# A graph network's last stage on one Trainium2 core: counts gathered one tile further ahead, and tile 0's mean and rows and the last mean transposed by TensorE

## The reference

```python
gates = softmax(x @ gate_W + gate_b)
top_v, top_i = top_k(gates, 2)
def sage_conv(h, W_l, b_l, W_r):
    aggr = segment_sum(h[src], dst) * inv_deg
    return aggr @ W_l + b_l + h @ W_r
for e in range(4):
    h = x
    for l in range(2):
        h = relu(sage_conv(h, Wl[e, l], bl[e, l], Wr[e, l]))
    expert_outs.append(h)
out = sum of the two chosen experts' h, each times its gate
```

## Time and profile before

| | |
|---|---|
| median of three runs | 757.63 us |
| lowest and highest | 754.64, 758.64 us |
| the profiled execution's own time | 759.32 us |
| its span in the trace | 757.6 us (757.57) |
| TensorE matmul busy | 722.2 us, 95% |
| VectorE busy | 434.0 us, 57% |
| ScalarE busy | 408.7 us, 54% |
| GpSimd busy | 183.4 us, 24% |
| last stage | from 482.8 us to the end |

### The profile page before, as it was taken

The page is one execution under the profiler, slowest core; times in us unless marked ns, Lnnn a source line. Parts: engine busy times, 40 slices in busy tenths (PEclk is TensorE's granted clock), DMA queues, the critical chain, the costliest instruction groups (busy, mean ns, idle before and its releaser), DMA issues.

```text
span 757.6 us, 12027 instructions
## 1 busy us (share of the span) xinstructions
PE 722.2 (95%) x3562; PEld 583.4 (77%) x3562; DVE 434.0 (57%) x1073; ACT 408.7 (54%) x927; POOL 183.4 (24%) x204
## 2 busy tenths in 40 slices
PE   5899999999999999999999999978999999999994
PEld 3589977888888887777777777756888788887783
DVE  8899889998842548522624424386444444453431
ACT  6956678776642523312413313357677767776771
POOL 4000000000000102831100100226555555655511
PEclk9999999999999999999999999999999999999997
DMA  9000001111501447799698692499434994439940
GB/s 214 27 3 3 4 3 32 37 34 46 158 2 56 113 133 251 202 350 346 209 369 309 224 338 96 138 252 327 99 75 93 261 347 97 88 71 232 310 126 6
DMA packets 46444, 115.19 MB, mean 152 GB/s; under 512 B 8340, under 2 KB 8552, under 8 KB 46361
## 3 DMA queue, kind: packets, MB, share of 16 engines
q1 hardware_dynamic: 28581, 77.60, 32.0%
q0 software_dynamic: 9136, 19.65, 11.5%
q10 hardware_dynamic: 8644, 16.86, 6.8%
HBM read 64.89 MB, written 50.08 MB: 152 GB/s over the span
## 4 chain that ended last, share of the span: by engine, by line
PE 82%; DMA 6%; DVE 5%; ACT 3%; issue 2%; POOL 0%; DVEq 0%; ACTq 0%; POOLq 0%
PE ps L1760 14%; PE ps L1761 14%; PE ps L1762 14%; DMA crow<-c_d,rec 6%; PE ps L2162 5%; PE ps L2161 4%; PE ps L1962 3%; PE ps L1956 3%; PE ps L2029 3%; PE ps L2030 3%; PE ps L1957 3%; PE ps L1837 3%; ACT agn L1097 1%; PE ps L2092 1%; PE ps L1900 1%
## 5 line engine op out<-in xcount | busy, mean ns | idle before, releaser
L1097 ACT ACTIVATE agn<-ps,rec 32x128 f32<-32x128 f32 x368 | 132.4, 360 | 43.0 <-PE ps L2162 38.6
L1040 ACT ACTIVATE slots<-he_t 125x512 fp32r<-125x512 f32 x40 | 25.4, 635 | 150.9 <-DVE he_t L1563 148.7
L2162 PE MATMUL ps<-slots,CTs 125*128 x230 | 90.0, 391 | 0.0
L1563 DVE TENSOR_TENSOR he_t<-ps,b_b 125x512 f32<-125x512 f32 x40 | 27.5, 690 | 105.4 <-PE ps L1762 72.2
L726 POOL DMA_INDIRECT hrow<-t_d,piece_i x80 | 75.9, 949 | 33.5 <-issue 24.1
L2161 PE MATMUL ps<-slots,CTs 125*128 x207 | 80.6, 390 | 0.0
L1723 DVE TENSOR_TENSOR tm<-ps,b_b 128x512 f32<-128x512 f32 x23 | 15.9, 691 | 85.6 <-PE ps L1762 85.5
L1760 PE MATMUL ps<-W,agT_hi 128*125 128x512 f32 x160 | 63.5, 397 | 0.0
L1760 PE MATMUL ps<-W,h2T_hi 128*125 128x512 f32 x160 | 63.4, 396 | 0.0
L1762 PE MATMUL ps<-W,agT_lo 128*125 128x512 f32 x160 | 63.3, 396 | 0.0
L1761 PE MATMUL ps<-W,agT_hi 128*125 128x512 f32 x160 | 63.2, 395 | 0.0
(11 more groups left out here) (306 smaller groups left out, 1671.5 us busy)
## 6 DMA issues: line engine op xcount, KB each, us to landing
he_d<-slots SPq DMA_DIRECT2D x30, 448.0 KB
slots<-he_d SPq DMA_DIRECT2D x30, 448.0 KB
w_d<-slots SPq DMA_DIRECT2D x3, 4096.0 KB, 19.2
slots<-w_d SPq DMA_DIRECT2D x24, 512.0 KB
t_d<-he_t SPq DMA_DIRECT2D x40, 224.0 KB
raw<-in_L_gnn_Wl ACTq DMA_DIRECT2D x4, 1024.0 KB, 8.3
raw<-in_L_gnn_Wr ACTq DMA_DIRECT2D x4, 1024.0 KB, 5.6
slots<-in_L_gnn_Wl ACTq DMA_DIRECT2D x4, 1024.0 KB, 9.7
```

Source lines behind the costliest of these rows:

```text
L1097: last = a.activation(agn[32 * r:32 * r + 32, q, :], ps[n, 3 + i % 2, 128 * r:128 * r + 128], ACT.Copy, scale=rec[n, i, 4:5])
L2162: last = mm(o, CTs[:, t, :], part(k, P, t * 1024 + D, P), start=False, stop=t == T - 1)
```

## The change

Three things. (1) The gather of counts runs four tiles ahead in GpSimd's loop instead of three; the one of tile 3 is made before the loop. (2) The tiles in BY_PE, the first and the last, have their mean turned by TensorE: ScalarE writes agn in one instruction, four fp32 transposes (`turn_means`) put it into PSUM bank 5, and aggT is made from there. Tile 0's hidden rows are copied by VectorE into the plain order and turned by four transposes (`turn_hidden`) into bank 7. Tile 0's transposes stand within and behind neighbours(1), the last tile's within transformed(21). (3) A new signal, own_done, counts the tiles whose own products are over; heT may then be overwritten, where it waited for the whole tile before. The making of aggT waits for the whole tile in its stead.

```diff
--- before.py
+++ after.py
@@ -307,6 +307,7 @@
         CTl = at("CTl", [P, T, S], F32R, 187360)
         heT_b, aggT_b = (at(n, [128, 2, KC, S], F32R, 192480 + 4096 * k) for k, n in enumerate(("heT", "aggT")))
         agn = at("agn", [128, RQ, KC * 32], F32, 200672)
+        BY_PE = (0, NT - 1)
         assert 200672 + 2048 <= row_at
         heT, aggT = ([b[:, k] for k in range(2)] for b in (heT_b, aggT_b))
 
@@ -349,10 +350,11 @@
         (out_stored,) = signals("out_stored")
         crow_in = signals("crow_in0 crow_in1 crow_in2")
         hrow_in = signals("hrow_in0 hrow_in1 hrow_in2")
+        (own_done,) = signals("own_done")
         (crow_turned, cts_ready, ctl_ready, hrow_used, heT_hi_ready, heT_lo_ready, agg_done, agn_ready, agn_turned,
-         aggT_hi_ready, aggT_lo_ready, tm_ready, tg_ready, settled) = signals(
+         aggT_hi_ready, aggT_lo_ready, tm_ready, tg_ready, agg_turned) = signals(
             "crow_turned cts_ready ctl_ready hrow_used heT_hi_ready heT_lo_ready agg_done agn_ready agn_turned "
-            "aggT_hi_ready aggT_lo_ready tm_ready tg_ready settled")
+            "aggT_hi_ready aggT_lo_ready tm_ready tg_ready agg_turned")
 
         consts, pool_step, dve_step = signals("consts pool_step dve_step")
 
@@ -742,12 +744,14 @@
                 gather_hidden(i)
             pool.wait_ge(*pre_ready(NE * T))
             gather_hidden(2)
+            pool.wait_ge(*crow_turned(3))
+            gather_counts(3)
             pool.wait_ge(*x2_out(32))
             pool.wait_ge(*table_ready(1))
             for i in range(NT):
-                if i + 3 < NT:
-                    pool.wait_ge(*crow_turned(3 * (i + 1)))
-                    gather_counts(i + 3)
+                if i + 4 < NT:
+                    pool.wait_ge(*crow_turned(3 * (i + 2)))
+                    gather_counts(i + 4)
                 if i + HB < NT:
                     pool.wait_ge(*hrow_used(i + 1))
                     gather_hidden(i + HB)
@@ -1079,8 +1083,13 @@
             act.wait_ge(*l1_done(NE * T))
 
             def turned_high(i):
+                if i == 0:
+                    act.wait_ge(*agg_turned(2))
+                    a.activation(heT[0], ps[:, 7, :].rearrange("p (c n) -> p c n", n=S), ACT.Relu
+                                 ).then_inc(heT_hi_ready.sem, 1)
+                    return
                 act.wait_ge(*hrow_used(i + 1))
-                act.wait_ge(*tiles_done(i))
+                act.wait_ge(*(own_done(i - 1) if i > 1 else tiles_done(1)))
                 a.activation(heT[0], hT_f[:].rearrange("p (k n) -> p k n", k=KC), ACT.Relu).then_inc(heT_hi_ready.sem, 1)
 
             def gated(i):
@@ -1091,6 +1100,10 @@
 
             def mean(i):
                 act.wait_ge(*agg_done(i + 1))
+                if i in BY_PE:
+                    a.activation(quartered(by_row(agn)), in_quarters(ps[:, 3 + i % 2, :]), ACT.Copy, scale=rec[:, i, 4:5]
+                                 ).then_inc(agn_ready.sem, 1)
+                    return
                 for q in range(RQ):
                     for r in range(RQ):
                         n = slice(32 * q, 32 * q + 32)
@@ -1099,18 +1112,23 @@
                 last.then_inc(agn_ready.sem, 1)
 
             def mean_high(i):
-                act.wait_ge(*agn_turned(i + 1))
-                copy(aggT[0], aT_f[:].rearrange("p (k n) -> p k n", k=KC)).then_inc(aggT_hi_ready.sem, 1)
+                if i in BY_PE:
+                    act.wait_ge(*agg_turned(1 if i == 0 else 3))
+                else:
+                    act.wait_ge(*agn_turned(i))
+                if i > 0:
+                    act.wait_ge(*tiles_done(i))
+                whole = ps[:, 5, :] if i in BY_PE else aT_f[:]
+                copy(aggT[0], whole.rearrange("p (k n) -> p k n", k=KC)).then_inc(aggT_hi_ready.sem, 1)
 
             mean(0)
             mean_high(0)
-            for i in range(NT):
-                if i == 0:
-                    turned_high(0)
-                else:
-                    turned_high(i)
-                    gated(i - 1)
-                    mean_high(i)
+            turned_high(0)
+            mean(1)
+            for i in range(1, NT):
+                turned_high(i)
+                gated(i - 1)
+                mean_high(i)
                 if i + 1 < NT:
                     mean(i + 1)
             gated(NT - 1)
@@ -1684,14 +1702,19 @@
 
             def turned_low(i):
                 dve.wait_ge(*heT_hi_ready(i + 1))
-                v.scalar_tensor_tensor(heT[1], hT_f[:].rearrange("p (k n) -> p k n", k=KC), 0.0, f32(heT[0]), ALU.max, ALU.subtract
+                if i > 0:
+                    dve.wait_ge(*(own_done(i - 1) if i > 1 else tiles_done(1)))
+                whole = hT_f[:] if i > 0 else ps[:, 7, :]
+                v.scalar_tensor_tensor(heT[1], whole.rearrange("p (k n) -> p k n", k=KC), 0.0, f32(heT[0]), ALU.max, ALU.subtract
                                        ).then_inc(heT_lo_ready.sem, 1)
 
             def turn_hidden(i):
 
                 dve.wait_ge(*hrow_in[i % HB](16 + 16 * RQ * (i // HB)))
-                if i > 0:
-                    dve.wait_ge(*heT_lo_ready(i))
+                if i == 0:
+                    v.tensor_copy(quartered(hT_f[:]), in_quarters(by_row(hrow[0]))).then_inc(hrow_used.sem, 1)
+                    return
+                dve.wait_ge(*heT_lo_ready(i))
                 if i >= HB:
                     last = v.transpose(by_pair(hT_f[:]), hrow[i % HB][:].rearrange("p q (k a) -> p q k a", k=KC))
                 else:
@@ -1704,13 +1727,13 @@
 
             def mean_low(i):
                 dve.wait_ge(*aggT_hi_ready(i + 1))
-                v.tensor_tensor(aggT[1], aT_f[:].rearrange("p (c n) -> p c n", n=S), f32(aggT[0]),
+                whole = ps[:, 5, :] if i in BY_PE else aT_f[:]
+                v.tensor_tensor(aggT[1], whole.rearrange("p (c n) -> p c n", n=S), f32(aggT[0]),
                                 ALU.subtract).then_inc(aggT_lo_ready.sem, 1)
 
             def turn_mean(i):
                 dve.wait_ge(*agn_ready(i + 1))
-                if i > 0:
-                    dve.wait_ge(*aggT_lo_ready(i))
+                dve.wait_ge(*aggT_lo_ready(i))
                 v.transpose(by_pair(aT_f[:]), agn[:].rearrange("p q (k a) -> p q k a", k=KC)).then_inc(agn_turned.sem, 1)
 
             def biased(i):
@@ -1728,7 +1751,6 @@
             counts_low(0)
             counts_in(1)
             counts_low(1)
-            turn_mean(0)
             mean_low(0)
             turn_hidden(0)
             turned_low(0)
@@ -1739,7 +1761,8 @@
                 turned_low(i)
                 if i + 1 < NT:
                     counts_low(i + 1)
-                turn_mean(i)
+                if i not in BY_PE:
+                    turn_mean(i)
                 mean_low(i)
                 if i + 2 < NT:
                     counts_in(i + 2)
@@ -2160,7 +2183,24 @@
                     if t > 0:
                         mm(o, CTs[:, t, :], part(k, P, t * 1024, P), start=False, stop=False)
                     last = mm(o, CTs[:, t, :], part(k, P, t * 1024 + D, P), start=False, stop=t == T - 1)
+                    if i == 1 and t == T // 2:
+                        turn_means(0)
                 last.then_inc(agg_done.sem, 1)
+
+            def turn_means(i):
+                pe.wait_ge(*agn_ready(i + 1))
+                if i == 0:
+                    pe.wait_ge(*pre_ready((NE - 1) * T + GROUPS[-1][1] + 1))
+                for c in range(KC):
+                    last = nc.tensor.transpose(ps[:, 5, c * S:(c + 1) * S], agn[:, c, :], ident[:])
+                last.then_inc(agg_turned.sem, 1)
+
+            def turn_hidden():
+
+                pe.wait_ge(*hrow_used(1))
+                for c in range(KC):
+                    last = nc.tensor.transpose(ps[:, 7, c * S:(c + 1) * S], hT_f[:, c * 128:(c + 1) * 128], ident[:])
+                last.then_inc(agg_turned.sem, 1)
 
             def transformed(i, k, w2_here):
 
@@ -2177,6 +2217,10 @@
                         at_w = (T + w + c) * 1024
                         last = three(o, hi[:, c, :], lo[:, c, :], part(k, 128, at_w, 128), part(k, 128, at_w + D, 128),
                                      j == 0 and c == 0, j == 1 and c == KC - 1)
+                        if i > 0 and j == 0 and c == KC - 1:
+                            last.then_inc(own_done.sem, 1)
+                        if i == NT - 2 and j == 0 and c == 2:
+                            turn_means(NT - 1)
                 last.then_inc(tiles_done.sem, 1)
 
             k, he_here, w2_here = slot_of(0)
@@ -2187,6 +2231,8 @@
                 if i + 1 < NT:
                     k, he_here, w2_here = slot_of(i + 1)
                     neighbours(i + 1, k, he_here)
+                if i == 0:
+                    turn_hidden()
                 if i + 2 < NT:
                     turn_rows(i + 2)
                 transformed(i, *here)
```

## The result

The changed kernel takes 744.07 us (median of four, 744.05 to 745.49) against 757.13 before (754.64 to 758.64): the ratio is 0.9835, with a 95% interval of 0.9806 to 0.9865. Timed a second time it took 743.99 against 757.74, ratio 0.9814 (0.9790 to 0.9838); five of these six executions lie at 743.95 to 744.02, one at 746.34. The profiled execution took 744.08 us with a span of 742.3; the span of before was 757.57.

What follows compares the result with a forecast made beforehand. TensorE's clock was taken as nearly full, so time could be won only where it stands still or runs slowly. Middle -7.8, head -3.7, tail +0.2 gave -11.3 us, from the median 757.63 to 746.3, range 743.8 to 749.5.

Steps and rivals of the forecast that it cites:

- first rival: In the tail, TensorE keeps the full clock behind its wait: -1.5 us, so 744.8; chance 0.22.
- the likeliest case: The forecast itself: 746.3 us, with a range of its own of 745.3 to 747.5; chance 0.58.
- The middle, -7.8: Tile 3 to 22: counts gathered a tile further ahead win 5.3 of waits, 1.5 of slow clock, 1.0 of restarts.
- third rival: Count gathers: the queue, not the issue, is the limit; only head and tail remain, -3.5, 754.1 us; chance 0.07.
- The head, -3.7: Tile 0 turned by TensorE: own products no longer wait for heT and end 3.5 to 3.9 us earlier.
- the wait for the copied hidden rows: Head: after neighbours(1) TensorE waits some 0.4 us for DVE's copy, taken as 0.5 us, ending at 494.4.
- The tail, +0.2: Last tile: four transposes on the path add 0.43 us, the wait for heT's low part shrinks by 0.22.
- I leave the slow stretch behind it in: Tail: idle time of 2.0 us becomes 1.8, so the slow stretch of 1.5 us behind it was assumed to stay.
- DVE at tile 1: Next in line in the head: heT low at 505.0, wanted at 506.7; holds with 1.7 us in hand.
- GpSimd's loop: Middle: under weight loads the loop takes 12.1 us, falls back 5.2 us, within 9.9 us of room.
- The slower rival: GpSimd's loop becomes the bound in the three loads; a loop of 14.2 us loses the gain; chance 0.03.
- transposes don't count as activity: Head: by this a slow stretch could follow the turns from 494.2 on, +1.5 us, 747.8; rival, chance 0.10.

Runs made afterwards that it cites:

- counts alone: The kernel before with only the counts gathered a tile further ahead: 750.35 us, ratio 0.9911.
- all but the counts: The changed kernel with the counts gathered three tiles ahead as before: 749.76 us, ratio 0.9905.
- tile 0's mean alone: The changed kernel with tile 0's hidden rows turned by VectorE in 16 pieces as before, only its mean through TensorE: 747.80 us, ratio 0.9861.
- without own_done: The changed kernel with ScalarE waiting for the whole tile before writing heT high, as before: 744.09 us, ratio 0.9810.
- the two edits together: The changed kernel with heT low ahead of tm in the last tile, and ScalarE waiting for the whole tile before: 744.07 us, ratio 0.9824.
- the last mean as before: The changed kernel with the last tile's mean made in 16 pieces and turned by VectorE as before, own_done kept: 745.27 us, ratio 0.9847.

## Why the prediction was right

It forecast 746.3 us in 743.8 to 749.5; measured 744.07. The outcome is that of its first rival (the tail keeps the full clock, 744.8, chance 0.22), not of the likeliest case.

- *The middle, -7.8*: the mechanism is shown by the counts alone. All periods are 10.79. Its size came from one execution, and the trace of the counts alone agrees with it to 0.1 us; by the times it is 5.4 to 6.7 (4.5 to 8.9 with the noise), and 5.0 on top of the head. The price includes the slow stretch behind the longest wait, which didn't come in all but the counts. That experiment also shows the third rival's price to be off: head and tail without the counts were put at 3.5 and brought 6.0 between medians and 7.2 by the ratio, and in the traces the middle is shorter by 3.2 with them too, 1.5 of it the slow stretch.
- *The head, -3.7*: measured -4.15 in the profiled pair, and the 0.3 between tile 2 and tile 3 besides (11.07 in counts alone, 10.78 in tile 0's mean alone). The step mis-sized is the wait for the copied hidden rows, put at 0.4 us: the copy took 0.42 and not 0.5, VectorE began it 0.61 behind the start of aggT low and not 0.69, and TensorE followed its end by 0.05. Then there was no wait at all. What the sum left out is that the head's wait could bring a slow stretch before the change, as it did in counts alone and in tile 0's mean alone; it took the one trace with 3.17 us and full clock for the rule. How often before has one there isn't shown.
- *The tail, +0.2*: +0.45 for the transposes (0.43 predicted) and -0.31 for the wait (-0.22). Without the last mean's turn the fast executions take the same time, as the sum said.
- *"I leave the slow stretch behind it in"*: this is the step that failed. Six traces have this wait at 1.7 us (the changed kernel twice, all but the counts, tile 0's mean alone, without own_done, and the two edits together), and no slow stretch follows it in any. The prediction weighed a wait shorter by 0.2 us as no change, and gave this rival 0.22. It is worth 1.5 of the 2.2 us by which the forecast was high. Why the clock stays full there isn't shown: in the trace of the last mean as before it stayed full behind 2.0 us too.
- *The whole*: without the 1.4 us at 43 us the profiled pair gives -13.8 against the forecast's -11.3: 0.45 and 0.3 from the head, 1.7 from the tail (-1.5 against +0.2). The medians give -13.1. That the number fell just inside the range owes something to luck: the range's lower end was drawn for the first rival.
- *Cover*: DVE at tile 1 (heT low from 502.07, own products from 504.69), GpSimd's loop (11.7 us at most) and the gathers held as worked out. The slower rival's loop of 14.2 us never came near.
- By the Trainium skill ("TensorE: Matmul & The Clock Gate", Part 4: PE-mode transpose) transposes don't count as activity in the way matmuls do. The trace doesn't go against it and doesn't show it: the head has two groups of turns within 1.1 us (492.87 to 493.92) and stays at full clock.

## What to carry to other kernels

A gather behind a queue in order is made early enough by its place in that queue: measure issue to use against the worst landing, not the median (10.9 us against 11.8 here), and one tile more ended all waits. A signal that frees a buffer early pays only if each engine of the chain can act on it: look for what stands in front of the step on the next engine too. When a standstill of TensorE is priced, a slow stretch behind it belongs to the price as a chance, and several executions say more of it than one trace.

## What the runs showed of the hardware

Waits of TensorE in the last stage, and the clock behind them, in the eleven traces: of those of 1.80 us or less none was followed by a slow stretch; of the eight of 2.0 to 3.2 us six were (2.00, 2.00, 2.58, 2.79, 3.14, 3.17) and two were not (2.0 in the last mean as before, 3.17 in the earlier trace rows). The same wait in the same place thus comes out both ways. One stretch costs 1.5 us, as worked out from the earlier trace rows.

A slow stretch also came at 43 us, behind small products and a standstill of 1.06 to 1.17 us, in the traces of before, of all but the counts, and without own_done, and not in the other eight, three of which had a standstill of 1.16 or 1.17 there and five one of 0.25 to 0.57. It costs some 1.4 us. With it the times of one kernel stand in steps: 744.0 and 745.4 for the changed kernel and its near kin; the one execution at 745.4 of which there is a trace, of the kernel without own_done, has its stretch there. What decides at 43 us wasn't tried.
